# Decoder kernel: each engine gets its own order of the steps in the two late attention blocks

## What is computed

```python
x = layernorm(x + L0_attn(x))          # stage A: softmax attention with a convolution of the values
x = layernorm(x + L0_xattn(x, ctx))    # stage B: cosine similarities with the context
x = layernorm(x + L0_ffn(x))           # stage C: four wide linear layers
x = layernorm(x + L1_attn(x))          # stage D: causal linear attention, 16 heads of 16, 64 relu features
x = layernorm(x + L1_xattn(x, ctx))    # stage E: softmax cross attention, 16 heads of 16
x = layernorm(x + L1_ffn(x))           # stage F: router, top 2 of 8 experts, gelu
```

## Time and profile before

| | |
|---|---|
| time, median of 3 runs | 1481.47 us (1478.37 to 1487.52) |
| span of the profiled execution | 1473.3 us, first to last instruction |
| TensorE busy | 1311.8 us (89%) |
| VectorE busy | 911.7 us (62%) |
| ScalarE busy | 573.1 us (39%) |
| GpSimd busy | 795.9 us (54%) |
| mean granted TensorE clock | 0.940 of full speed |

### The profile page before, as it was taken

How to read it: one execution, slowest core, us unless ns; L and a number is a source line. 1 busy time by engine, 2 the same in 40 slices (tenths; PEclk the granted TensorE clock), 3 DMA queues, 4 the chain that set the end, 5 groups by cost and what they waited for, 6 DMA issues and landing times.

```text
span 1473.3 us, 23156 instructions
## 1 busy us (share of the span) xinstructions
PE 1311.8 (89%) x9073; PEld 1113.5 (76%) x9073; DVE 911.7 (62%) x1729; ACT 573.1 (39%) x1172; POOL 795.9 (54%) x761
## 2 busy tenths in 40 slices
PE   6998999999999999988899888987884699999980
PEld 6997788888888888866666666666653699999980
DVE  4656622632442262234687787777884699999966
ACT  3566311211121121124344444433342477777742
POOL 4444566666576576523232344535565347888831
PEclk9998999999999999999899999988885799999995
DMA  5101233233343233213324324235531755666605
GB/s 177 39 18 39 73 99 122 86 101 101 107 136 100 86 100 100 75 42 83 108 64 121 94 68 111 52 110 134 144 144 36 227 203 209 231 234 227 223 15 165
DMA packets 63101, 169.53 MB, mean 115 GB/s; under 512 B 11029, under 2 KB 30735, under 8 KB 55056
## 3 DMA queue, kind: packets, MB, share of 16 engines
q1 hardware_dynamic: 52432, 122.19, 27.8%
q0 software_dynamic: 10560, 45.86, 8.8%
HBM read 138.57 MB, written 33.38 MB: 117 GB/s over the span
## 4 chain that ended last, share of the span: by engine, by line
PE 71%; DVE 16%; ACT 3%; issue 3%; POOL 2%; DMA 2%; SPq 1%; ACTq 0%; POOLq 0%; DVEq 0%
PE bank L410 16%; PE bank L412 15%; PE bank L411 15%; PE bank L1297 9%; PE bank L418 4%; PE bank L1056 3%; PE bank L1137 3%; DVE topE L1809 3%; DVE shiftE L1816 3%; DVE topE L1811 1%; PE bank L1213 1%; ACT x_tok L458 1%; PE bank L1124 1%; PE bank L1192 1%; DVE x_tok L1977 1%
## 5 line engine op out<-in xcount | busy, mean ns | idle before, releaser
L1680 DVE CAST hid_hi<-bank 128x512 fp32r<-128x512 f32 x96 | 66.4, 691 | 252.1 <-ACT bank L1412 251.0
L552 POOL TENSOR_TENSOR wpiece_lo<-wraw,wpiece_hi 128x1024 fp32r<-128x1024 f32 x88 | 211.1, 2398 | 7.3
L410 PE MATMUL bank<-hid_hi,wpiece_lo 128*128 128x512 f32 x512 | 199.3, 389 | 0.0
L412 PE MATMUL bank<-hid_hi,wpiece_hi 128*128 128x512 f32 x512 | 199.2, 389 | 0.0
L411 PE MATMUL bank<-hid_lo,wpiece_hi 128*128 128x512 f32 x512 | 199.2, 389 | 0.0
L550 POOL TENSOR_SCALAR wpiece_hi<-wraw 128x1024 fp32r<-128x1024 f32 x88 | 94.1, 1069 | 154.7 <-PE bank L412 126.7
L1412 ACT ACTIVATE bank<-bank,ffn_scales 128x512 f32<-128x512 f32 x64 | 42.4, 662 | 301.5 <-PE bank L412 301.5
L1498 ACT ACTIVATE staging<-bank 128x512 f32<-128x512 f32 x128 | 70.0, 599 | 129.4 <-PE bank L1213 117.7
L412 PEld LDWEIGHTS bank<-hid_hi,wpiece_hi 128*128 128x128 f32 x512 | 96.1, 188 | 20.1
L410 PEld LDWEIGHTS bank<-hid_hi,wpiece_lo 128*128 128x128 f32 x512 | 96.1, 188 | 20.1
L411 PEld LDWEIGHTS bank<-hid_lo,wpiece_hi 128*128 128x128 f32 x512 | 96.1, 188 | 20.0
(11 more groups left out here) (342 smaller groups left out, 3696.9 us busy)
## 6 DMA issues: line engine op xcount, KB each, us to landing
wraw<-in_C_w SPq DMA_DIRECT2D x88, 512.0 KB, 3.6
w2raw<-in_F_w SPq DMA_DIRECT2D x8, 1152.0 KB, 7.2
w1raw<-in_F_w SPq DMA_DIRECT2D x8, 1028.0 KB, 7.4
split_qk<-qk_hi SPq DMA_DIRECT2D x64, 128.0 KB, 3.8
xt_lo<-split_qk SPq DMA_DIRECT2D x8, 1024.0 KB, 6.4
xt_hi<-split_qk SPq DMA_DIRECT2D x8, 1024.0 KB, 5.1
split_qk<-qk_lo SPq DMA_DIRECT2D x32, 128.0 KB
split_qk<-ctx_raw SPq DMA_DIRECT2D x32, 128.0 KB, 3.8
```

Source lines behind the costliest of these rows:

```text
L410: pe.e.matmul(o, sl, mh, start=start and i == 0, stop=False)
L412: made = pe.e.matmul(o, sh, mh, start=False, stop=stop and i == n - 1)
L552: pool.e.tensor_tensor(pair[1], raw, f(pair[0]), ALU.subtract).then_inc(done, 1)
```

## The change

The five engines no longer share one list: each has its own, `DE["pe"]`, `DE["act"]` and so on. Two tables alter the items. `LATER` moves a step by rounds, for all engines: cross scores (`PAIR` 0) and E's keys (`EPRE` 1) one round later; the second linear scores (`QUAD` 2), D's query projection (`DPRE` 0), the first head transposes of D and the second of E, and the start of E's output projection (`EFIN` 0) one round earlier. `PLACE` gives a step another priority in its round, for all engines or for one: weighted values of E (`PAIR` 2), the second linear scores and E's output projection stand first, then D's weighted values; D's output projection, power and transposes stand last. So in even rounds TensorE has D's weighted values, cross scores, transposes, first linear scores; in odd rounds E's weighted values, the second linear scores of the next quad, cross scores, transposes, features. GpSimd's clip comes after its slot writes of steps 1 and 2 of a round. The last two sequences start E at d + 20 like the others. The PSUM banks are handed out by TensorE's list.

```diff
-def de_steps():
-
-
+PLACE = {
+    "all": {("DFIN", 1): 7, ("DFIN", 2): 4.5, ("DFIN", 3): 7, ("DPRE", 1): 0.5, ("EDR", 0, 0): -0.5, ("EFIN", 1): -2,
+            ("EFIN", 2): 1.5, ("EFIN", 3): 0.5, ("EFIN", 6): -0.5, ("PAIR", 2): -2, ("QUAD", 2): -2, ("QUAD", 3):
+            -0.5},
+    "pe": {("EDR", 1, 0): 4.5, ("EPRE", 1): 0.5, ("EPRE", 3): 2.5},
+    "act": {("DFIN", 3): 1.5, ("EPRE", 1): -0.5},
+    "dve": {("EFIN", 2): -1},
+    "pool": {("PAIR", 1): 2.5, ("SLOTS", 1): 1.5, ("SLOTS", 2): 2.5},
+}
+LATER = {
+    "all": {("DDR", 0, 0): -1, ("DPRE", 0): -1, ("EDR", 1, 0): -1, ("EFIN", 0): -1, ("EPRE", 1): 1, ("PAIR", 0): 1,
+            ("QUAD", 2): -1},
+}
+
+def de_items():
     items = [(3, 5, "CN", (b,), 1) for b in range(B - BPS, B)]
     for b in range(B):
         d = 4 + PAIRS * b
-        e = d + (20 if b < B - 2 else 22)
+        e = d + (20 if b < B - 2 else 20)
...
+    return items
+
+
+def de_steps(engine):
+    order = []
+    for n, (first, prio, name, args, at) in enumerate(de_items()):
+        for step, r in enumerate(range(at) if isinstance(at, int) else at):
+            q = prio if isinstance(prio, int) or isinstance(prio, float) else prio[step]
+            key = (name, args[1], step) if name in ("DDR", "EDR") else (name, step)
+            for who in ("all", engine):
+                r += LATER.get(who, {}).get(key, 0)
+                q = PLACE.get(who, {}).get(key, q)
+            order.append((first + r, q, first, n, name, step, args))
+    return [x[4:] for x in sorted(order)]
...
-AB, DE, FS, GS = ab_steps(), de_steps(), f_steps(), g_steps()
+AB, FS, GS = ab_steps(), f_steps(), g_steps()
+DE = {e: de_steps(e) for e in ("pe", "act", "dve", "pool", "sp")}
...
-    for name, step, args in DE:
+    for name, step, args in DE["pe"]:
```

More of the change, by code:

```diff
@@ L136, in g_steps @@
     return in_rounds([(b, 0, "SUM", (b,), 3) for b in range(B)])
-AB, DE, FS, GS = ab_steps(), de_steps(), f_steps(), g_steps()
+AB, FS, GS = ab_steps(), f_steps(), g_steps()
+DE = {e: de_steps(e) for e in ("pe", "act", "dve", "pool", "sp")}
 def bank_order():
-    every, low, held, upper, wide = range(8), range(6), range(6, 8), range(4, 8), range(8, 10)
+    every, low, held, upper = range(8), range(6), range(6, 8), range(4, 8)
+    wide_f, wide_s, wide_e = range(8, 10), range(8, 10), range(8, 10)
     out = []
@@ L168, in bank_order @@
         elif name == "QUAD" and step == 0:
-            out.append((("D", "f", *args), wide))
+            out.append((("D", "f", *args), wide_f))
         elif name == "QUAD" and step < 3:
-            out.append((("D", "s", *args, step - 1), wide))
+            out.append((("D", "s", *args, step - 1), wide_s))
         elif name == "QUAD":
@@ L178, in bank_order @@
         elif name == "PAIR" and step == 0:
-            out.append((("E", "s", *args), wide))
+            out.append((("E", "s", *args), wide_e))
         elif name == "PAIR" and step == 1:
@@ L640, in pool_program @@
                 pool.e.memset(v[:, :, :, DH:DH + 1], 1.0).then_inc(s_vone, 1)
-            for name, step, args in DE:
+            for name, step, args in DE["pool"]:
                 if name == "DPRE" and step == 0 and args[0] == 1:
@@ L861, in stack_heads @@
                      held.rearrange("i r (d j) s -> (i r d) (j s)", j=4), l_qk[b % 2])
-            for name, step, args in DE:
+            for name, step, args in DE["sp"]:
                 b = args[0]
@@ L1434, in finish @@
                     ln_apply(act, stage, b, resid[b % 2 if stage == "D" else 2])
-            for name, step, args in DE:
+            for name, step, args in DE["act"]:
                 if name == "CN":
@@ L1773, in finish @@
                     ln_scale(dve, stage, b)
-            for name, step, args in DE:
+            for name, step, args in DE["dve"]:
                 if name == "CN":
```

1 line of the change is left out of this document (removed).

## The result

| | before | after |
|---|---|---|
| time, median of 4 runs each, same chip | 1483.40 us (1478.37 to 1487.52) | 1434.63 us (1428.04 to 1440.13) |
| ratio | | 0.9671, 95% interval 0.9631 to 0.9711 |
| span of the profiled execution | 1473.3 us | 1431.1 us |
| mean granted TensorE clock | 0.940 | 0.944 |

The change makes the kernel 3.3% faster: 48.8 us by the medians, 42.2 us by the two profiled spans. The forecast was 1442.5 us, from a gain of 39 us. The profiled execution of after took 1432.86 us, 1.8 us more than its span. So most of the 8.2 us that I carried over from span to median was spread between executions, and before's profiled one was a quick one. I compare spans with spans. One run of the kernel before in the first group of experiments took 4373.36 us; it is left out of that group's median.

The account below looks back on a forecast made before the run. TensorE, waiting for double-width PSUM banks that VectorE drains, bounds the mixed stretches; VectorE bounds the E-only rounds. Gains 9 + 19 + 5 + 6 = 39 us; 1473.3 - 39 + 8.2 = 1442.5 us, range 1422 to 1467 (8 in 10).

Parts of the forecast that it names:

- Part 1: Mixed stretches of D and E: reordered scores and weighted values remove most TensorE waits; gain 19 us, bounds 6 and 35.
- Part 2: First rounds: later keys and cross scores cover two TensorE waits and a clock loss; gain 9 us, bounds 2 and 14.
- Part 3: Last two sequences' E starts two rounds earlier, filling VectorE's hole; gain 5 us, bounds -4 and 9.
- all of that can go: Hole from 1024.2 to 1038.9: cross scores of sequence 6 fill VectorE's 8.6 us of idle time.
- Part 4: End of the last sequence: last cross scores to last weighted values take 8.5 us, not 14.3; gain 6 us, bounds 3 and 7.
- up to 2.3 us if a clip is late: Cost of GpSimd's slot writes moving ahead of a clip in two rounds of eight; otherwise nothing.
- A chain of its own and only starts earlier: After the last weighted values: block gathers, experts and output keep their time.
- A (the wait only moves): Rival: VectorE late by 1 us four times a stretch; total gain 21 us, 1460.5 us; chance 0.20.
- B (line 1840 grows): Rival: VectorE's four-column operation, line 1811 before, lengthens; at mean 1.6 us the time is 1510 us; chance 0.05.
- 64 us per us of mean: Rival B's price: the four-column line runs 64 times in VectorE's chain, each further us costing up to 64 us.
- C (the early start hurts): Rival: E-only rounds fall to 1.2 GHz, part 3 gives -12 us; total gain 11 us, 1470.5 us; chance 0.08.
- D, the full ceiling: Rival: stretches of 48.5 us and no clock losses; total gain 61 us, 1420.5 us; chance 0.07.

Follow-up runs that it names:

- group 1: First group of experiments; its changed kernel is the same changed kernel run again, nothing altered, as yardstick on another chip: 1423.09 us, ratio 0.9656 to the kernel before.

## Why the prediction was right

**The bound, held.** Two double-width banks used in turn, with the second linear scores too close behind the cross scores. Moved alone, they give 17 to 18 us (the last run); put back, the wait returns at 16.6 us in 24 rounds. The changed kernel has 1.2 us of it in the stretch of the earlier trace rows, "under 2 us" as said. What the prediction didn't have is that the moves need each other. It priced part 1 as a whole, so this alone cost no accuracy; priced move by move it would have been wrong.

**The size was too small, and the near hit is in part luck.** The forecast gain was 39 us. The medians give 48.8 us on one chip and 51 on the other, the two profiled spans 42.2 and 54.5. The profiled execution of after holds a stall and a fall of the clock worth 6.3 us (last section) and a gather slower by 3.3, both missing in the second execution; without them the sum of the parts would not have come so near. Parts 1 and 2 were sized too small, the others too large.

**Part 1 (19 us forecast, 24.0 and 31.4 measured).** I left 4.0 us of loss in each stretch; measured are 3.5 in the mean, 17.3 over five. So 2.7 of the 5 us of difference are loss below the 20 that I left. The other 2.3 are in TensorE's work at full speed, which I took as constant: the busy time less the clock's part is 228.9 us in the earlier trace rows and 226.6 in the windows after. The stretches are cut at round starts, and some steps have moved by a round, so some work may have changed sides; eight fewer matmuls are counted in the windows after. Forecast for a stretch was 50 to 53 us; five rows have 46.0, 49.3, 51.2, 55.4 and 42.0, and in the execution of group 1 46.0, 49.3, 50.2, 49.3 and 41.8. There the loss is about 9 us in all, where I left 20: that is the term of the sum that was sized wrong. The clock, which I asked to be 0.97 or more, is 0.91 and 0.96 in the last two stretches of after, and 1.00 and 0.96 there. VectorE is busy 212 of 244 us, 87%, as said.

**Part 2 (9 us forecast, 14.5 measured, over its bound of 14).** From 636 us to the first mixed stretch TensorE is idle 15.7 us of 120.3 in the earlier trace rows and 4.8 of 105.8 after: 10.9 us, where I took 6. The two waits of the earlier trace rows went whole, 6.6 us. The other 4.3 are short waits that I hadn't looked for: by the waits of that time, for features 3.0 us before and 1.1 after, a second case for the context's split of 1.3, stands without a cause 2.9 and 1.0, and against them a new one of 1.4 for VectorE's masks. The busy time fell by 3.6 us with the same work, where I took 3 for the clock; its level is 1.00 from 706.2 to 741.8, against 0.88. Cross scores put back brought the DMA wait back (4.00 us), so that cover is shown; the keys' wait was not tried by itself.

**Part 3 (5 us forecast, 3.1 in the trace, none by the start put back): the step least borne out.** The trace reads nearly as predicted: the hole gives 6.8 us, where all 8.6 us of its idle time were to go, and the E-only rounds cost 3.7 (3.5 forecast), with TensorE waiting 9.4 us before its transposes and VectorE busy 56.8 of 60.8 us. But the kernel that starts at d + 22 again is as fast. What failed is the step from "all of that can go" to a gain. With the later start GpSimd is through with the slot writes when the last clips come, TensorE stands 1.04 us and not 4.40 or 2.73, its clock doesn't fall, and the end is some 5 to 7 us shorter. With the clip first, where the slot writes are out of the way, the early start did pay 8 us by the medians; the spans show 1.4 of them. The E-only rounds are bound by VectorE, and whether the cross scores are near or far only says who waits.

**Part 4 (6 us forecast, 3.6 measured; 10.7 us in place of 8.5).** The chain of scores, VectorE, transposes, exponential went as said, but I counted one slot write before the clip. The last two clips stand behind four token writes and two code writes of about 1.0 us with 0.30 between. I had written that the new place on GpSimd's list costs "up to 2.3 us if a clip is late"; the clip was late, and clip first again gives 3.0 us from last transposes to last weighted values, in place of 6.7 and 4.7: a cost of 3.7 and 1.7 us.

**Behind the last weighted values: -3.6 us in one execution, -0.4 in the other.** In after, from GpSimd's first token write of sequence 7 to the transposes of the first gathered block pass 17.7 us (1089.49 to 1107.20), against 14.1 before (1134.70 to 1148.76): SyncE issues the gather 1.5 us later behind them, and it takes 2.2 us longer to land. GpSimd writes the codes of sequence 6 until 1089.2, right up to these token writes, where before it was done 1.0 us ahead of them. That isn't the cause by itself: the codes stand as close (0.30 us) in the changed kernel of group 1 and in the one with the second scores back, and there the same way takes 14.4 and 14.3 us. In the ten other executions with 0.30 us between them it takes 14.3 to 17.1 us, in the three with 1.0 us 14.1 to 14.5, so it may have a part. "A chain of its own and only starts earlier" held in one of the two executions; what makes the gather slow in the other is open.

**The rivals.** A (the wait only moves) didn't come: before line 1221 TensorE waits nowhere in the stretch of the earlier trace rows. It is what the second scores alone give (5.7 us before line 1192, 1459 us), where cross scores and the engines' own orders stay as they were. B (line 1840 grows) didn't come: its mean is 433 and 479 ns in two executions of the changed kernel and 487 before, its longest case 1.5 us in place of 2.8. Leaving the line out gives 9 to 11 us for 31 us of work, 0.3 us per us, so my price of 64 us per us of mean was three times too high, as far as taking away tells of adding. C (the early start hurts) was right in that it wasn't worth anything beside the `"pool"` entries, and wrong in the -12 us. D, the full ceiling with a gain of 61 us, wasn't reached: with 1.00 in all 24 rounds the changed kernel of group 1 gained 51. Its 1423.09 us lie near D's 1420.5, but that chip's kernel before is quicker too, 1474.53 where D starts from 1481.47.

The sum of my terms was 39, of the measured ones 14.5 + 24.0 + 3.1 + 3.6 - 3.6 = 41.6 to the first gathered block, 42.2 by the spans. The other 4.7 us of the 7.9 between 1442.5 and 1434.63 are the carried-over difference between span and median, 8.2 us where after has 3.5.

## What to carry to other kernels

Where in-order engines share a few buffers in turn, list the uses in order and measure how much other work lies between a use and the use two places on; a wait there can be removed by moving a step into the gap. Making the drain cheaper as well (line 1840 out, 31 us off VectorE) gave only 9 to 11 us more. Price such a reordering as a whole stretch followed and not move by move: here the parts taken back singly cost 30, 25 and 9 us and the one tried alone gave 17, of 51. Follow every queue past the last buffer, the one that looks idle too: with slot writes of 1 us each ahead of the last clip the earlier start was worth nothing, and with the clip ahead of them 8 us by the medians. And take a second trace of the same program before you explain a part of a difference: 6.3 and 3.3 us of the first one were missing in the second.

## What was unexpected of the hardware

**A stall without a cause, and then half a clock.** In after's profiled execution, in the middle of eight matmuls that form one group:

```profile
910.68 0.48 PE L1166 MATMUL bank<-feat 64*128 64x256 f32 x1
912.51 0.37 PE L1166 MATMUL bank<-feat 64*128 64x256 f32 x1 [1.35 <-issue]
913.90 1.51 PE L1166 MATMUL bank<-feat 64*128 64x256 f32 x4 [1.02 <-issue]
```

Nothing that the profile shows holds them, and the group, with two more matmuls from 915.19 on, takes 5.1 us in place of its 0.92. The granted clock falls with it. Windows of after around it, and the same eight rounds (first transposes of sequence 4's E to those of sequence 5's) in after and in the changed kernel of group 1:

```profile
908.00:918.00 10.00, 7.50 (x52) 5.49 (x51) 4.07 (x9) 2.03 (x8) 5.66 (x6) 0.75 0.54 79
918.00:928.00 10.00, 10.00 (x77) 6.86 (x76) 7.12 (x21) 5.11 (x10) 3.72 (x8) 0.74 0.13 21
...
905.90:958.10 52.20, 49.52 (x424) 36.10 (x424) 40.02 (x79) 22.44 (x47) 25.79 (x33) 0.90 0.37 101
```

```profile
902.20:948.10 45.90, 44.55 (x423) 32.73 (x422) 41.77 (x79) 22.62 (x48) 25.74 (x33) 1.00 0.37 114
```

The same program needs 52.2 us there in one execution and 45.9 in the other, 6.3 us that belong to no part of the change. They are half of the 12.3 us between the two spans, 1431.1 and 1418.8. What stalled the group is open.

The Trainium skill (TensorE: Matmul & The Clock Gate, "A second HAM failure mode: psum-queue depth-cycling") has the clock swing when TensorE idles briefly and often between groups as it goes through the PSUM banks. In these rounds of after TensorE has no wait for PSUM at all and the clock falls with a stall of another kind, so small waits for PSUM did not make this fall; the stretches in which the waits of the earlier trace rows stood had 1.00 as well.

**A four-column instruction waits for GpSimd's arithmetic.** Line 1840 lasts 0.17 us at best and 1.44 at worst in one execution of after, at a median of 0.19; in the changed kernel of group 1 its median is 0.26. Put beside GpSimd's timeline, its 64 cases fall apart. The longest one of after:

```profile
1033.20 2.06 POOL L699 TENSOR_SCALAR staging<-staging 128x1024 f32<-128x1024 f32 x2
1033.85 1.44 DVE L1840 TENSOR_SCALAR topE<-topE 128x4 f32<-128x4 f32 x1
```

It ends at 1035.29, GpSimd's clip at 1035.26. In after 29 cases last over 0.3 us, and all 29 end within 0.15 us of the end of an arithmetic instruction of GpSimd; in the changed kernel of group 1 31 of 32 do, in before 20 of 23. The 17 cases of after in which GpSimd does nothing last 0.17 us each, the 11 that meet only an indirect DMA at most 0.24, and the 7 left overlap GpSimd's arithmetic by 0.26 us or less. The 2.79 us of the earlier trace rows lie across four instructions of GpSimd that follow each other closely, and end 0.03 us after the last. Line 1845, which reads PSUM, lasts 1.223 to 1.226 us in all its 64 cases. So the small instruction stands while GpSimd computes. With the new order such meetings became more frequent, 28 and 31 cases over 0.4 us against 21 before, though the longest is shorter.

The Trainium skill (SBUF — State Buffer, "SBUF: two separate sides") names a port pair that VectorE and GpSimd share and that one of them holds for a whole instruction. The cases above agree with it, 29 of 29 in after; that it is this pair and not another thing that the two engines share, no run here shows.
